# A branch prefetch hint at the top of the loops of four engines, in a gathered adapter and layer-norm kernel

## The reference

```
h = einsum('bsh,bhk->bsk', x, W_down[role]) + b_down[role]      # 1024 -> 512
h = gelu(h, approximate=False)
u = einsum('bsk,bkh->bsh', h, W_up[role]) + b_up[role]          # 512 -> 1024
y = x + u
yn = (y - mean(y)) * rsqrt(var(y) + 1e-5)
out = yn * gamma[role] + beta[role]
```

## Time and profile before

| | before |
|---|---|
| median of 3 runs | 1422.99 us (1422.77 to 1423.64) |
| span of the profiled execution, first to last instruction | 1420.9 us |
| TensorE matmuls, busy | 1405.4 us (99%) |
| VectorE, busy | 1202.9 us (85%) |
| ScalarE, busy | 780.8 us (55%) |
| GpSimd, busy | 200.1 us (14%) |
| DMA, mean | 200 GB/s |

### The profile page before, as it was taken

How to read it: one execution, slowest core, us unless ns; L and a number is a source line. 1 busy time by engine, 2 the same in 40 slices (tenths; PEclk the granted TensorE clock), 3 DMA queues, 4 the chain that set the end, 5 groups by cost and what they waited for, 6 DMA issues and landing times.

```text
span 1420.9 us, 32269 instructions
## 1 busy us (share of the span) xinstructions
PE 1405.4 (99%) x6175; PEld 1156.2 (81%) x6176; DVE 1202.9 (85%) x1456; ACT 780.8 (55%) x2053; POOL 200.1 (14%) x300
## 2 busy tenths in 40 slices
PE   8999999999999999999999999999999999999997
PEld 6888888888888888888888888888888888888885
DVE  8798988888888888888888898888888888888887
ACT  5555555555555555555555555555555555555555
POOL 4376311100000000000000376311100000000000
PEclk9999999999999999999999999999999999999999
DMA  8678877766666666666666778777766666666664
GB/s 222 187 224 229 217 213 204 205 197 201 184 192 197 196 181 195 197 196 183 190 201 194 212 225 232 223 199 207 207 200 182 196 199 190 185 193 202 189 186 149
DMA packets 208870, 283.52 MB, mean 200 GB/s; under 512 B 25791, under 2 KB 155584, under 8 KB 208846
## 3 DMA queue, kind: packets, MB, share of 16 engines
q1 hardware_dynamic: 201870, 269.60, 63.3%
q0 software_dynamic: 5888, 12.07, 4.8%
q10 hardware_dynamic: 1088, 1.57, 0.4%
HBM read 183.27 MB, written 99.88 MB: 199 GB/s over the span
## 4 chain that ended last, share of the span: by engine, by line
PE 96%; DVE 1%; DMA 1%; ACT 1%; issue 0%; SPq 0%; DVEq 0%; ACTq 0%
PE p_down L1058 16%; PE p_down L1060 16%; PE p_up L1058 16%; PE p_down L1059 16%; PE p_up L1059 16%; PE p_up L1060 16%; DMA h_dram<-h 0%; DMA row<-in_L_cond_W_down 0%; DVE row L823 0%; DMA x_quad<-in_x 0%; ACT factor L635 0%; ACT rstd L637 0%; DVE p_hT L765 0%; DVE row L982 0%; PE p_hT L1054 0%
## 5 line engine op out<-in xcount | busy, mean ns | idle before, releaser
L1058 PE MATMUL p_down<-wd_hi,xT_hi 128*128 x1012 | 395.7, 391 | 0.5 <-DVE wd_lo L723 0.3
L1060 PE MATMUL p_down<-wd_hi,xT_lo 128*128 x1012 | 394.0, 389 | 0.0
L1059 PE MATMUL p_down<-wd_lo,xT_hi 128*128 x1012 | 393.9, 389 | 0.0
L1058 PE MATMUL p_up<-wu_hi,hT_hi 128*128 x1008 | 392.8, 390 | 0.0
L1059 PE MATMUL p_up<-wu_lo,hT_hi 128*128 x1008 | 392.3, 389 | 0.0
L1060 PE MATMUL p_up<-wu_hi,hT_lo 128*128 x1008 | 392.3, 389 | 0.0
L576 ACT ACTIVATE hT_hi<-p_hT 128x512 fp32r<-128x512 f32 x126 | 75.5, 599 | 440.4 <-DVE p_hT L765 437.0
L785 DVE SCALAR_TENSOR_TENSOR row<-p_up,row 128x1024 f32<-128x1024 f32 x126 | 154.2, 1224 | 180.6 <-PE p_up L1060 148.2
L1058 PEld LDWEIGHTS p_down<-wd_hi,xT_hi 128*128 128x128 f32 x1012 | 189.9, 188 | 45.9 <-issue 6.7
L1058 PEld LDWEIGHTS p_up<-wu_hi,hT_hi 128*128 128x128 f32 x1008 | 189.2, 188 | 41.7 <-issue 2.0
L1060 PEld LDWEIGHTS p_down<-wd_hi,xT_lo 128*128 128x128 f32 x1012 | 190.0, 188 | 39.6
(11 more groups left out here) (174 smaller groups left out, 957.7 us busy)
## 6 DMA issues: line engine op xcount, KB each, us to landing
x_quad<-in_x SPq DMA_DIRECT2D x510, 128.0 KB, 3.6
row<-in_x SPq DMA_DIRECT2D x126, 512.0 KB, 4.1
out<-row SPq DMA_DIRECT2D x126, 512.0 KB, 2.8
h_dram<-h SPq DMA_DIRECT2D x125, 256.0 KB, 4.3
h_quad<-h_dram SPq DMA_DIRECT2D x500, 64.0 KB, 2.0
w_raw<-in_L_cond_W_down POOLq DMA_DIRECT2D x64, 64.0 KB, 3.2
w_raw<-in_L_cond_W_up POOLq DMA_DIRECT2D x64, 64.0 KB, 3.7
row<-in_L_cond_W_up SPq DMA_DIRECT2D x16, 128.0 KB, 3.8
```

The source lines that it names most:

```text
L1058: pe.matmul(dst, a_hi, w_hi, start=first, stop=False)
L1059: pe.matmul(dst, a_hi, w_lo, start=False, stop=False)
L1060: return pe.matmul(dst, a_lo, w_hi, start=False, stop=last)
```

## The change

The loop of `pipeline` is made with the more general call, which allows one more argument. It runs on the same one engine, over the same range.

```
             for i in range(first, HEAD):
                 body(i - i % RING, i % RING)
-            with eng.Fori(HEAD, B - RING, RING) as i:
+            with nc.Fori(HEAD, B - RING, RING, engines=[eng.engine], hint_back_edge=True) as i:
                 for k in range(RING):
                     body(i, k)
             for i in range(B - RING, last + 1):
                 body(i - i % RING, i % RING)
```

## The result

The changed kernel takes **1430.8 us** (median of 5 runs, 1429.6 to 1431.9) against 1422.8 (5 runs, 1421.4 to 1423.6): ratio **1.0059**, 95% interval 1.0049 to 1.0070. It is 8.0 us slower, where the forecast was 1425.5 us, 2.5 us slower, with a range that ended at 1429.5.

The account below looks back on a forecast made before the run. TensorE was taken to bound the kernel, its turns 3.8 us above the array's floor. Base 1422.99 us plus 2.5 us for the hint, with the branch, ScalarE and the sync engine at 0, gave 1425.5 us; range 1421.0 to 1429.5.

Parts of the forecast that it names:

- The base and the bound: Measured base 1422.99 us; TensorE bounds, its 28 turns only 3.8 us above the array's floor, put down to its sequencer.
- The price of the hint in the loop: At the turn's top, a hint delays VectorE's sequencer 0.10 us, reaching the end in 25 of 28 turns: +2.5 us.
- three signs of being wrong: VectorE's gap behind its branch under 0.2 us, a hint over 0.15 us, or late issues in bodies three and four.
- The rule that VectorE's delay goes through one for one: In a turn with a late issue, VectorE's 0.10 us delay in body one costs the array the same time.
- on TensorE its like is no longer: At the turn's top, a hint on TensorE takes no longer than the 0.10 us taken for VectorE's.
- ScalarE and the sync engine at 0: Hints on these two cost 0, covered by waits of 3.5 us ahead of L576 and 2.7 us at L286.
- The branch: VectorE's taken branch resumes in about 0.3 us; taken as unchanged by the hint, since nothing is fetched from 260 to 920 us.
- The hint makes the sequencer fetch its target again each turn: Rival, behind TensorE's branch: refetching stalls the sequencer, 17 to 46 us slower, some 1450 us; chance 0.06.
- Nothing measurable: Rival, at the turn's top: the hint is lost among table reads or waits, 1423.0 us; chance 0.2.
- cheaper branch: Rival, between VectorE's branch and next instruction: the 0.3 us shrinks, 2.7 us won, 1420.3 us; chance 0.14.

Follow-up runs that it names:

- lean_pe: Kernel before, no hint, with TensorE's table reads moved to where its sequencer waits anyway, ahead of the wait for h: 1420.2 us, ratio 0.9983.
- lean_both: As lean_pe, and VectorE reads each parameter entry once per turn and only where it is used: ratio 1.0005 to the kernel before.
- h_pe_b: Repeat of h_pe, the changed kernel with the hint armed on TensorE alone: ratio 1.0018 to the kernel before.
- h_pe: Changed kernel with the hint armed on TensorE alone: ratio 1.0021 to the kernel before.
- h_dve: Changed kernel with the hint armed on VectorE alone: ratio 1.0028 to the kernel before.
- hr_dve: Hint on VectorE alone, its outcome in a register (not taken in the last turn), two more register operations per turn: ratio 1.0024 to the kernel before.
- h_sp_act: Changed kernel with the hint armed on the sync engine and ScalarE alone: ratio 1.0008 to the kernel before.
- long_hint: As long_plain, 16 bodies per turn, with the change's hints: 1438.5 us, ratio 1.0101 to the kernel before.
- long_plain: Kernel before with turns of 16 bodies instead of 4, no hint: 1452.8 us, ratio 1.0225.

## Why the prediction was wrong

**The base and the bound: right.** TensorE was the bound, and its turns had 3.8 us above the floor, or 4.1 with the step of 0.2266 us as it is written; the rows from 199.67 to 212.36 us are 57 matmuls, 56 steps, and not 56 matmuls. lean_pe took 2.1 us of it back by touching nothing but TensorE's reads, so at least half of it was sequencer time. The rest was not shown: lean_both, which went for VectorE's share, won nothing.

**The price of the hint in the loop: the sum about right, its terms not.** I took 0.10 us on VectorE in 25 of 28 turns, +2.5 us; the turns grew by 3.0. That they come so near is in part luck. The trace of before has a late issue in 21 turns and not in 25, and five of its 31 are ahead of body one's down product, where the forecast saw none; in the changed kernel it is 26 turns, with 18 late issues ahead of body one's down product and 24 ahead of body two's, and none in bodies three and four. But VectorE's hint costs its sequencer only 0.02 us. The hint and the step behind it are 39 + 47 ns, and in return the gap between branch and next instruction falls from 260 to 195 ns, which I had taken as unchanged. A gap under 0.2 us was one of my three signs of being wrong, and it came true. TensorE's costs 0.11 us, with nothing in return. By engine the turns grew by 1.8 to 2.2 us (h_pe_b, h_pe) and 1.1 (h_dve), the last within what two profiles of one kernel can differ by. The rule that VectorE's delay goes through one for one held (hr_dve: 0.15 us in, 0.11 to 0.13 out); "on TensorE its like is no longer", said of 0.10 us, held nearly. But most of the loss came by TensorE's hint, while the sum had been worked out from VectorE's.

**ScalarE and the sync engine at 0: right in the loop, wrong behind it.** The turns of h_sp_act are those of before. The rest is 1.6 us longer when these two are hinted alone, and in the changed kernel that vanishes behind VectorE's pause.

**The step that failed is "The branch".** There I said that a taken branch resumes in 0.3 us and that nothing is fetched for it from 260 to 920 us, and took the branch as unchanged. That nothing is fetched was true of the 28 taken branches and left out the 29th execution. The last branch falls through, and the question for it is who fetches what comes next. The packets that the hint displaces come in the first turn, outside the stretch that I looked at; no row of before could have told that a hint displaces them, but those rows would have raised the question. In place of the nothing that I had there the runs show 4.9 us behind the loop. In the changed kernel 2.7 of it is the array's pause behind VectorE's hole of 3.8 us, some 1.5 the low clock after the pause and 0.7 the rest; VectorE's hint alone costs 3.0 there, the sync engine's and ScalarE's alone 1.6, TensorE's nothing. Without these 4.9 us the kernel would have been 3.1 us slower, where the forecast said 2.5.

**The rivals.** "The hint makes the sequencer fetch its target again each turn" was the nearest, since it blamed the fetcher, but it had the wrong moment: the hint makes no packet move in the turns, the harm is the missing blocks at the end. "Nothing measurable" and "cheaper branch" fall; the second has a grain of truth in VectorE's gap, 65 ns shorter.

## What to carry to other kernels

In these runs a branch hint paid only by moving a fetch: use it where the trace shows the fetch, as a branch of microseconds (4.4 to 6.0 us here, in turns of 16 bodies), and not where the branch takes 0.2 us and no instruction packet moves in the loop. It promises the branch of the last turn too, and the code behind the loop can pay for that: 3.0 us by VectorE's hint here, nothing by TensorE's, and nothing in the long turns or with the hint in mid-turn. Look at the first and the last turn, not only at the middle. Where the bounding engine waits for "issue", ask what its sequencer does at that point, and move table reads to a place where it waits anyway.

## What was not expected of the hardware

- A pause of the array of 2.9 us at the exit was followed by 3 us at the 1.2 GHz level, and cost 1.5 us beyond itself. In h_dve a pause of 2.65 us was not. The length alone doesn't decide it: in long_hint one of 2.35 us (from 266.1 us) was followed by the low level, in long_plain one of 3.88 us (from 446.0 us) was not. The windows behind these two, in this order:

```profile
269.40:272.60 3.20, 3.20 (x9) 2.44 (x8) 3.08 (x4) 1.72 (x3) 0.54 (x1) 0.50 0.86 179
```

```profile
450.20:453.40 3.20, 3.20 (x15) 2.63 (x15) 2.91 (x5) 0.76 (x2) 0.00 (x0) 1.00 0.41 127
```

- Instruction packets that came in a loop's first turn, at 104 to 127 us, seem to have served when the loop ended at 1353 us: VectorE's five table reads behind the loop go on without a hole in the kernel before, and have one of 3.8 us where the packets are missing.
- On VectorE a hint shortens the gap behind a taken branch whose target was at hand, 260 to 195 ns, and on the sync engine and ScalarE alike (257 to 202, 192 to 159), but TensorE's branch gets 16 ns longer.
- A hint of 31 ns on TensorE, 0.11 us with its gaps, costs as much as 0.31 us of plain waits at the same place, for a reason that stays open.
